# Gating 28 of 32 token tiles inside the last body, and a projection taken slot by slot

## The reference

```python
xn = _layernorm(x, axis=-1)
s = _L0_attn_ref(xn, L0_attn_W_qkv, L0_attn_W_out)
g = _silu(_L0_ffn_ref(xn, L0_ffn_gate_w, L0_ffn_gate_b, L0_ffn_w1, L0_ffn_b1, L0_ffn_w2, L0_ffn_b2))
x = x + s * g
return x
```

## Time and profile before

| | |
|---|---|
| median of 3 runs | 1272.3 us (1271.93 to 1272.8) |
| the profiled execution | 1278.0 us |
| its span in the trace | 1276.1 us |
| TensorE busy | 1160.4 us, 91% of the span |
| VectorE, ScalarE, GpSimd busy | 1015.3, 935.9, 879.8 us |
| mean granted TensorE clock | 0.965 of full |

### The profile page before, as it was taken

How to read it: one execution, slowest core, us unless ns; L and a number is a source line. 1 busy time by engine, 2 the same in 40 slices (tenths; PEclk the granted TensorE clock), 3 DMA queues, 4 the chain that set the end, 5 groups by cost and what they waited for, 6 DMA issues and landing times.

```text
span 1276.1 us, 54245 instructions
## 1 busy us (share of the span) xinstructions
PE 1160.4 (91%) x17610; PEld 917.6 (72%) x17611; DVE 1015.3 (80%) x3105; ACT 935.9 (73%) x1791; POOL 879.8 (69%) x1080
## 2 busy tenths in 40 slices
PE   1559999999999999998999779999999999999992
PEld 0327777787787887777777657777777777777772
DVE  8758888888888888885666558888888888888874
ACT  1338888888888888885555468888888888888882
POOL 9128888888888888882000058888888888888883
PEclk9669999999999999999999889999999999999996
DMA  6416666666666666674332366665555555555553
GB/s 217 164 39 131 145 146 148 145 143 141 146 145 143 143 145 142 145 136 78 81 78 75 87 144 140 138 135 132 132 132 132 132 132 133 132 132 132 132 116 83
DMA packets 286151, 164.92 MB, mean 129 GB/s; under 512 B 175010, under 2 KB 274690, under 8 KB 285444
## 3 DMA queue, kind: packets, MB, share of 16 engines
q1 hardware_dynamic: 281988, 155.63, 53.5%
q0 software_dynamic: 4096, 8.40, 2.4%
HBM read 15.76 MB, written 16.78 MB: 25 GB/s over the span
## 4 chain that ended last, share of the span: by engine, by line
PE 80%; DVE 6%; DMA 4%; issue 4%; ACT 3%; SPq 2%; POOL 0%; ACTq 0%; DVEq 0%; POOLq 0%
PE ps L874 11%; PE ps L848 11%; PE ps L776 8%; PE ps L777 7%; PE ps L778 7%; PE ps L878 6%; PE outs L905 6%; PE outs L909 6%; PE outs L907 5%; PE ps L875 4%; DMA k_st<-stage 3%; PE ps L881 2%; PE ps L857 2%; PE outs L777 1%; DVE mix L1227 1%
## 5 line engine op out<-in xcount | busy, mean ns | idle before, releaser
L737 POOL TENSOR_TENSOR t_lo<-stage 128x512 f16<-128x512 f32 x640 | 654.8, 1038 | 108.1 <-ACT stage L1106 102.2
L1281 DVE CUSTOM_DVE_ANT_0 stage<-ps,kmask 128x512 bf16<-128x512 f32 (+3 forms) x1024 | 467.2, 488 | 122.5 <-PE ps L848 103.3
L1106 ACT ACTIVATE stage<-ps,slope 128x512 f32<-128x512 f32 (+1 forms) x768 | 455.6, 619 | 117.4 <-PE ps L881 68.6
L874 PE MATMUL ps<-q_st,k_st 128*128 128x256 f16 (+3 forms) x1024 | 306.3, 302 | 10.6 <-ACT stage L1106 6.1
L905 PE MATMUL outs<-v_sp,stage 128*128 128x65 f16 x2560 | 282.6, 195 | 4.2 <-DVE stage L1311 2.8
L907 PE MATMUL outs<-v_sp,stage 128*128 128x64 f16 x2560 | 282.4, 194 | 0.0
L909 PE MATMUL outs<-v_sp,t_lo 128*128 128x65 f16 x2560 | 282.3, 194 | 0.0
L848 PE MATMUL ps<-k_st,stage 128*128 128x512 f16 (+3 forms) x1024 | 252.0, 303 | 13.3 <-DMA k_st<-stage 5.5
L905 PEld LDWEIGHTS outs<-v_sp,stage 128*128 128x128 bf16 x2560 | 238.5, 98 | 11.8 <-issue 4.0
L907 PEld LDWEIGHTS outs<-v_sp,stage 128*128 128x128 bf16 x2560 | 235.9, 98 | 9.1 <-issue 0.3
L909 PEld LDWEIGHTS outs<-v_sp,t_lo 128*128 128x128 f16 x2560 | 236.1, 98 | 0.0
(11 more groups left out here) (198 smaller groups left out, 2772.5 us busy)
## 6 DMA issues: line engine op xcount, KB each, us to landing
k_st<-stage SPq DMA_DIRECT2D x256, 128.0 KB, 2.4
q_st<-stage SPq DMA_DIRECT2D x256, 128.0 KB, 2.4
q_st<-stage SPq DMA_DIRECT2D x256, 64.0 KB, 2.1
k_st<-stage SPq DMA_DIRECT2D x128, 64.0 KB, 2.3
slot_y<-stage SPq DMA_DIRECT2D x40, 128.0 KB, 1.8
X<-in_L_attn_inputs SPq DMA_DIRECT2D x8, 512.0 KB, 6.1
slot_x<-att SPq DMA_DIRECT2D x2, 2048.0 KB, 8.7
wx_raw<-in_L_ffn_w SPq DMA_DIRECT2D x64, 64.0 KB
```

Source lines behind the costliest of these rows:

```text
L737: pool.tensor_tensor(t_lo[r], t_p[r], upper(t_p[r]), ALU.subtract).then_inc(s[f"lo{u % NG}"], 1)
L874: pe.matmul(d, k[:, 0, at], q[:, 0, seen], start=True, stop=False, skip_group_check=True)
L1106: e = act.activation(t_p[r][:, c0:c1], S_ps[u % 2][:, c0:c1], ACT.Exp, scale=slope[:, bass.ds(pair_index(n) * 2 * SLOTS + sl * 2 + h, 1)])
L1281: ins = dve.tensor_tensor_reduce(junk[h][:, c0:c0 + w], M_ps[h][:, c0:c0 + w], kmask[:, SEQ - w:SEQ], -1.0 / 1024, 3e38, ALU.add, ALU.min, ...
```

## The change

1. **Pieces.** The tiles are cut into three pieces, `PIECES`: tiles 0 to 13 and 14 to 27 (1792 columns each) and 28 to 31 (512).
2. **Silu in three.** ScalarE takes the first two pieces in `out_hi` of body 63's second slot, ahead of that task's waits and its copy, the third behind it. `silu` counts them.
3. **`finish`.** A new function multiplies `att` by the gate and adds it to `X` for a piece, on one engine. It waits for that piece's Silu, for `xend`, and for 56 accumulations (64 for the last piece). GpSimd does piece 0 behind its last low part. VectorE does piece 1 in `accumulate` of body 63, ahead of that task's wait for `op`, and piece 2 at the end. Each piece has a store of its own, in this order.
4. **The scale.** The factor 1/64 moves out of the finish into each accumulation, which becomes a scalar_tensor_tensor; the gating becomes a tensor_tensor.
5. **`project`.** It waits for the bank and `ta0`, takes the first slot's 12 products, waits for `ta1`, takes the second's 12. Only the first product of all opens the bank (`start`).

```diff
@@ -271,11 +271,11 @@
             scaled picked ranked routed zeros ready0 ready1 rhi sent0 sent1 got00 got01 got10 got11 weighed0 weighed1 added
             w_in w_hi w_lo xend
             xload0 xload1 hmm0 hmm1 gelu0 gelu1 hhi hlo0 hlo1 ymm yout ystore0 ystore1
-            gated rd0 rd1 nrm0 nrm1 op acc ta0 ta1 ah0 ah1 al0 al1 rows
+            gated0 gated1 gated2 rd0 rd1 nrm0 nrm1 op acc ta0 ta1 ah0 ah1 al0 al1 rows
             turnc0 turnc1 crow0 crow1 copied
             qst0 qst1 kst0 kst1 scales
             qmm0 qmm1 qh0 qh1 ql0 ql1 kmm kh kl vmm vh vl
-            finD finP outd""".split()
+            fin0 fin1 fin2 outd""".split()
         s = {n: sem("s_" + n) for n in names}
@@ -440,9 +440,25 @@
                 need(nc.tensor, last_reader + ("" if user[0] in "OKV" else user[1]), body + 1)
                 return
+        LAST = NT - QT
+        PIECES = [(0, LAST // 2), (LAST // 2, LAST), (LAST, NT)]
         def out_chunk(v, c):
-            return v[:, 8 * c:8 * c + 8, :].rearrange("p t d -> p (t d)")
+            t0, t1 = PIECES[c]
+            return v[:, t0:t1, :].rearrange("p t d -> p (t d)")
+        def finish(eng, c):
+            need(eng, "silu", c + 1)
+            eng.wait_ge(s["acc"], BODIES if c == 2 else BODIES - PAIRS)
+            eng.wait_ge(s["xend"], 64)
+            a, g, xx = (out_chunk(v, c) for v in (att, mix, X))
+            eng.tensor_tensor(a, a, g, ALU.mult).then_inc(s[f"gated{c}"], 1)
+            eng.wait_ge(s[f"gated{c}"], 1)
+            eng.tensor_tensor(xx, xx, a, ALU.add).then_inc(s[f"fin{c}"], 1)
         def round_of(j):
             sl, j = divmod(j, NR * 2)
@@ -591,10 +607,10 @@
             ot = out.rearrange("b (t p) d -> p (b t) d", p=P)
-            for c, name in ((0, "finP"), (2, "finD"), (1, "finP"), (3, "finD")):
-                sp.wait_ge(s[name], c % 2 + 1)
-                sp.dma_start(ot[:, 8 * c:8 * c + 8, :], X[:, 8 * c:8 * c + 8, :]).then_inc(s["outd"], 16)
-            sp.wait_ge(s["outd"], 64)
+            for c, (t0, t1) in enumerate(PIECES):
+                sp.wait_ge(s[f"fin{c}"], 1)
+                sp.dma_start(ot[:, t0:t1, :], X[:, t0:t1, :]).then_inc(s["outd"], 16)
+            sp.wait_ge(s["outd"], 16 * len(PIECES))
         @block.gpsimd
@@ -762,11 +778,7 @@
             enter_bodies("POOL", fetches, HALF, BODIES)
             run_bodies(pool, "POOL", fetches, HALF, BODIES)
             leave_bodies("POOL", fetches, HALF, BODIES)
-            pool.wait_ge(s["xend"], 64)
-            for c in range(2):
-                pool.wait_ge(s["gated"], c + 1)
-                xx = out_chunk(X, c)
-                pool.tensor_tensor(xx, xx, out_chunk(att, c), ALU.add).then_inc(s["finP"], 1)
+            finish(pool, 0)
         @block.tensor
@@ -912,18 +924,18 @@
             def project(n, par, _):
+                bank_free(n, "O0")
                 for sl in range(SLOTS):
                     need(pe, f"ta{sl}", (n + 1) * 16)
-                bank_free(n, "O0")
-                for t in range(QT):
-                    tok = slice(t * P, (t + 1) * P)
-                    for sl in range(SLOTS):
-                        j = bass.ds(pair_index(n) * SLOTS + sl, 1)
+                    j = bass.ds(pair_index(n) * SLOTS + sl, 1)
+                    for t in range(QT):
+                        tok = slice(t * P, (t + 1) * P)
                         mm = three(bank_of("O0")[:, tok], aT[par][sl][:, tok],
                                    aT[par][sl][:, (QT + t) * P:(QT + t + 1) * P],
                                    wo_hi[:, j, :].rearrange("p a d -> p (a d)"),
                                    wo_lo[:, j, :].rearrange("p a d -> p (a d)"),
-                                   start=(sl == 0), stop=(sl == SLOTS - 1))
+                                   start=(sl == 0 and t == 0), stop=(sl == SLOTS - 1), shared_bank=True)
                 mm.then_inc(s["op"], 1)
             tasks = {"Q": queries, "K": keys, "V": vals, "M": rough, "C": turn_shifts, "S": scores, "P": values,
@@ -1078,14 +1090,26 @@
                 act.activation(v_sp[par][:, :, V_HI:V_HI + SLOTS * DH], v_bank(),
                                ACT.Copy, scale=1.0 / WS).then_inc(s["vh"], 1)
+            def gates(c):
+                g = out_chunk(mix, c)
+                act.activation(g, g, ACT.Silu).then_inc(s["silu"], 1)
             def out_hi(n, _, sl):
+                final = isinstance(n, int) and (n, sl) == (BODIES - 1, 1)
+                if final:
+                    act.wait_ge(s["added"], NT)
+                    for c in range(2):
+                        gates(c)
                 act.wait_ge(s[f"nrm{sl}"], n + 1)
                 need(act, f"ta{sl}", n * 16)
                 if isinstance(n, int) and (n, sl) == (HALF, 0):
                     for k in range(2):
                         act.wait_ge(s[f"ystore{k}"], NBLK // 2 * 16)
                 act.copy(by_head(a16[sl][:, 0:SEQ]), values_of(sl)).then_inc(s[f"ah{sl}"], 1)
+                if final:
+                    gates(2)
             def shifts(n, _, sl):
@@ -1188,8 +1212,6 @@
             act.preload_act_table(ACT.Exp)
             run_bodies(act, "ACT", {**tasks, "F": weigh}, HALF, BODIES)
             leave_bodies("ACT", {**tasks, "F": weigh}, HALF, BODIES)
-            act.wait_ge(s["added"], NT)
-            act.activation(mix[:, :, :], mix[:, :, :], ACT.Silu).then_inc(s["silu"], 1)
         @block.vector
@@ -1322,9 +1344,12 @@
             def accumulate(n, _par, _):
+                if isinstance(n, int) and n == BODIES - 1:
+                    finish(dve, 1)
                 dve.wait_ge(s["op"], n + 1)
                 a = att[:, bass.ds(batch_index(n) * QT, QT), :].rearrange("p t d -> p (t d)")
-                dve.tensor_tensor(a, bank_of("O0")[:, :], a, ALU.add).then_inc(s["acc"], 1)
+                dve.scalar_tensor_tensor(out=a, in0=bank_of("O0")[:, :], scalar=1.0 / WS, in1=a, op0=ALU.mult,
+                                         op1=ALU.add).then_inc(s["acc"], 1)
             tasks = {"B": peaks, "Q": q_lo, "K": k_lo_part, "V": v_lo_part, "A": out_lo, "N": normalise,
                      "O": accumulate}
@@ -1411,16 +1436,7 @@
             leave_bodies("DVE", tasks, HALF, BODIES)
-            dve.wait_ge(s["silu"], 1)
-            dve.wait_ge(s["acc"], BODIES)
-            dve.wait_ge(s["xend"], 64)
-            for c in range(4):
-                a, g, xx = (out_chunk(v, c) for v in (att, mix, X))
-                dve.scalar_tensor_tensor(out=a, in0=a, scalar=1.0 / WS, in1=g, op0=ALU.mult, op1=ALU.mult)\
-                   .then_inc(s["gated"], 1)
-                if c >= 2:
-                    dve.wait_ge(s["gated"], c + 1)
-                    dve.tensor_tensor(xx, xx, a, ALU.add).then_inc(s["finD"], 1)
+            finish(dve, 2)
 _INS = ["L0_attn_inputs", "L0_attn_W_qkv", "L0_attn_W_out", "L0_ffn_gate_w", "L0_ffn_gate_b",
```

## The result

The changed kernel takes **1264.4 us** (median of 4 runs, 1261.9 to 1266.8) where the kernel before takes 1272.4 on the same chip (4 runs, 1271.9 to 1272.8): a ratio of 0.9937, with an interval of 0.9922 to 0.9951, so 8.0 us less (6.2 to 9.9). 9.5 were forecast.

What follows compares the result with a forecast made beforehand. It took TensorE (busy 29.98 of 30) to bound the middle and a serial chain the end. Tail 7.2 plus loops 2.3 made 9.5 us off 1272.3, so 1262.8 us, range 1260.2 to 1266.8.

Steps and rivals of the forecast that it cites:

- Step 1: Before body 63's last copy: table load and two Silu pieces (1.28 + 3.5) fill ScalarE's 4.71 us hole, delaying it 0.0 to 0.1.
- step 3: Body 63's projection: products end near 1257.7 instead of 1259.05, worth 1.3 us alone, costed at nothing as VectorE comes later.
- Step 2: Gating and adding 28 tiles: GpSimd (3.8 us an operation) and VectorE (1.95) alternate on the shared port, 1250.1 to 1261.65.
- C: Rival for the ending: no port turns, the other turn, or fast GpSimd; 1260.8, 1261.5 or 1259.5 us; chance 0.17 together.
- Step 4: Last piece on VectorE: accumulation 0.70 us, multiplication and addition of 512 columns 0.7 each, done at 1263.8.
- Step 5: Output: first store at 1259.75, 7.33 us of data, end at 1268.9 instead of 1276.1, so the tail gives 7.2 us.
- Step 6: The 64 accumulations as scalar_tensor_tensor: costs nothing, at most 3.6 us if all were on the path.
- Step 7: Projections in the loops: second slot's register work hides behind twelve products, 26 bodies x 0.09 = 2.3 us gained.
- Rival A: The loops give nothing, TensorE's time goes to a wait for k_st or an exponential: 1265.1 us, chance 0.20.
- Rival B: Mid-projection wait for `ta1` empties TensorE's queue, 0.17 us in each of 64 bodies: 1276.0 us, chance 0.04.
- Rival D: No overlap: GpSimd also holds body 63's normalisation, delaying copy, transpose and products; 1263.7 us with the loops, chance 0.05.

Runs made afterwards that it cites:

- e4_before_again: The kernel before, unchanged, profiled once more: 1275.1 us in one run.
- e3_four_pieces: Changed kernel with pieces of 10, 9, 9 and 4 tiles, one Silu ahead of the last copy, GpSimd only multiplying the first piece: 1266.5 us, 0.9917 of before.
- e2_no_turns: Changed kernel without GpSimd's multiplication and addition of piece 0: 1265.6 us in one run.
- e1_order_only: The kernel before with only the projection's order changed: 1275.6 us, 0.9986 of before.
- e1_finish_only: Changed kernel with the projection order of the kernel before: 1271.7 us, 0.9955 of before.
- e1_both_waits: Changed kernel with both transposes awaited at the projection's start, register work still moved: 1269.8 us, 0.9943 of before.
- e1_after_again: The changed kernel, unaltered, run again on another chip: 1271.0 us against 1278.1 of before, ratio 0.9948.
- e2_fewer_products: Changed kernel with the 8 wo_lo products left out of every projection (16 instead of 24): 1252.3 us, 0.9795 of before.

## Why the prediction was right, and where it was off

The time lies in its range, 1.6 us above the forecast. On the experiments' chips the gain is 6.6 and 5.6 us, with intervals (5.0 to 8.4 and 4.0 to 7.3) that leave the 9.5 out; that the first comparison came nearer to it, with 8.0, is not the sum's merit. Step by step:

- **Step 1, Silu in the hole.** Right in form: two pieces took 3.28 (3.5 counted), the load 1.28. But the hole of 4.71 was that of an execution with slow products. At full clock it is 3.25: e4_before_again and e3_four_pieces start the copy 3.26 behind the last exponential, the changed kernel 4.51 (1247.62 - 1243.11), so it can be 1.25 late. It cost nothing, for the reason given at step 3.
- **Step 2, the turns.** Right, in order and in length: GpSimd 3.98 and 3.82 (3.8 counted), VectorE 1.88 and 1.89 between the turns (1.95 counted), 12.8 from the last exponential to the first store (12.73). The rivals without turns, or with the other turn (C), are out; e2_no_turns shows what they would have looked like.
- **Step 3, the projection in two groups.** Costed at nothing in the tail, and it is nothing: 22.04, 21.99 and 21.98 with both orders. Alone, with the old ending, it was priced at 1.3. From the issue of the last transpose to the last accumulation it is 5.91 us in one profile of before (1259.07 - 1253.16) and 5.90 in the other, and 3.98 in e1_order_only, so 1.9 less. In that execution the last 12 products ran at full clock (steps of 0.057), in both of before at half (0.105); this accounts for 12 x 0.048 = 0.6, and 1.3 is left for the order. (The prediction's 0.114 a product holds the length of the last product; the steps are 0.105.)
- **Step 4.** The last accumulation, gating and addition are 0.68, 0.69 and 0.69, where 0.70 each were counted.
- **Step 5, the stores.** First store to end 9.19, forecast 9.13. The sum of steps 1 to 5 was off all the same, since it subtracts from a tail of before that is 29.08 in one execution and 27.63 in another: the gain is **5.6 to 7.1, not 7.2**. The new tail was forecast to a tenth; the old one was read from the slow end of what it varies over.
- **Step 6, the accumulation's other form.** Nothing, as taken: e1_finish_only has it and keeps the loops' old periods. By form (line, shape, count, busy us, mean ns), where the earlier trace rows have 688:

```profile
L1351 DVE SCALAR_TENSOR_TENSOR att<-ps,att 128x512 f32 x52 | 35.7, 687 | 0.0
```
- **Step 7, the loops. This is the step that failed**, by its size. The register work is hidden as it says; in a second-half body of the changed kernel, behind the third product:

```profile
1204.20 0.22 PE L788 MATMUL ps<-wo_hi,aT 128*128 x1
...
1204.26 0.22 PE L789 MATMUL ps<-wo_lo,aT 128*128 x1
```
The products step by 0.055 here where the earlier trace rows have 0.09 and 0.11. (Only the first step of a projection, with the first slot's own register work, stays at 0.12 as before.) In the mean over 25 bodies of before the two steps held 0.106 us more than the others, not 0.09. But the period falls by 0.052, for two steps elsewhere in the body grow by some 0.06, the first of `rough` and the first of `keys`. The step took busy 29.98 of 30 as proof that what TensorE saves shortens the run one for one, and it does not. And the first half, which the step left out because its products had no gap, loses 0.027 a body. 2.3 us shrink to 1.35 - 0.7 = 0.65, and the medians of two direct comparisons give 0.7 and 0.6. The cause that the step named is not enough either: with the register work moved and both waits kept (e1_both_waits) the gap ahead of the projection grows by as much as is saved, and the period is the old one. Why the products of `rough` and `keys` come late stays open.
- **Rival A** (the loops give nothing, 1265.1) is nearer to the net than the forecast, though by another way: both halves moved, against each other. **Rival B** (the wait in the middle costs) has its sign right in the first half, at 0.027 a body and not 0.17, and not by its mechanism: no gap opens behind the twelfth product. **Rival D** is out: VectorE's operations that read PSUM kept 0.68 to 0.70 beside GpSimd.

The corrected sum is 5.6 to 7.1 and 0.65, so 6.3 to 7.8; the three comparisons measured 8.0, 6.6 and 5.6, each with an interval of some 1.8 us to either side.

## What to carry to other kernels

When a tail is overlapped, forecast the new tail by its own chain, and take the old one from more than one execution: a wait that depends on the granted clock can make it 1.5 us longer in the one that was profiled. Where VectorE and GpSimd share elementwise work with two SBUF inputs, their times add up; give GpSimd one early piece and let the first store leave soon, in pieces that keep the stores running (17.2 us of tail instead of 22.0). An engine that is busy 99% in the profile need not be the bound: before a saving in a loop is multiplied by its bodies, take a known amount of that engine's work away and read the period of each loop. And compare periods on one chip: two profiles from different chips made 0.05 us a body look like 0.24.

## What was not expected of the hardware

- After the same 1.89 us of idle time, the same products ran at a granted clock of 0.50 to 1.00 in the mean, from one execution to the next. Which it is was not foreseeable from the rows ahead of it, and it moves the old ending by up to 1.5 us. In the last projection of the changed kernel's first profile the first group of 12 products ran at full clock and, after 1.72 us of idle time, the second at half (steps of 0.11); in e1_after_again the second group ran at full clock after the same 1.72 us.
- Programs that are the same take 1272.4 us on one chip and 1276.5 to 1278.1 on three others. In the traces of the changed kernel the difference lies in the second half's loop: its period is 15.66 on the first chip and 15.84 on the others, with 15.29 and 15.31 in the first half. It stands at three steps around the products of `rough`: to the first of them (0.034 instead of 0.077 us in the mean), from it to `keys` (0.22 instead of 0.31) and from the last of them to the scores (0.31 instead of 0.36). What differs there stays open.
- In a loop that takes TensorE's full time, 0.11 us less between the products of one group made the body shorter by 0.05 only, while 0.50 us less in the same group (e2_fewer_products) made it shorter by 0.52, and the delay at the first product of `rough` was gone again (0.034).
